# A hand-written TensorE order: both sums of a unit pair in even units, one place per unit for full-size work, D x u one unit later

## The chip, the cores and the metric

One core of a Trainium2 chip runs the kernel. The metric is the device time of one execution in microseconds (us). All arithmetic of the kernel is fp32.

## What is computed

The reference is a "macaron" block over x of shape (16, 512, 256): half a feed-forward layer, a selective state-space (Mamba-like) mixer, and half a feed-forward layer again. Cut to what matters here:

```python
x = x + 0.5 * ffn(layernorm(x))
# mixer: u = silu(conv(h @ Win[:, :512])), z = h @ Win[:, 512:], dt = softplus(u @ dt_w + dt_b)
#        Bt = u @ Bp, Ct = u @ Cp        (512 channels, 64 states per channel, 512 time steps)
def step(state, inp):
    x_t, dt_t, B_t, C_t = inp
    dA = jnp.exp(dt_t[:, :, None] * A[None])
    state = state * dA + (dt_t * x_t)[:, :, None] * B_t[:, None, :]
    y_t = jnp.einsum('bds,bs->bd', state, C_t)
    return (state, y_t)
y = (y + u * D) * silu(z)
x = x + (x_ + y @ Wout)
x = x + 0.5 * ffn(layernorm(x))
```

## The kernel before

**Units.** The mixer's state is walked in units. A unit is one tile of 128 channels with four of the 64 states, over all 512 time steps. A sequence of the batch has 64 units (`GN`), and 16 sequences follow one another. Units `n` and `n + 1` (`n` even) are a pair: the same four states for two neighbouring channel tiles. `HALF` is 32: the first 32 units serve channel tiles 0 and 1, the last 32 serve tiles 2 and 3. Each unit goes through four engines:

- ScalarE makes `dA` (L435), four exponentials of 128x512, into a ring of two.
- TensorE makes `pUB`, the product of dt x u and B, by 64x64 tiles (`force`, L687). It does so in two halves `i = 0, 1` of two states each; each half is 32 matmul records. There is one PSUM buffer per half, so half `i` of a unit may start only when VectorE has read half `i` of the unit before (`state_done`, L679).
- VectorE runs the recurrence (`tensor_tensor_scan`, L567): four scans per unit, two per half, each half waiting for `forced`. It writes `H`, a ring of four units.
- GpSimd multiplies `H` by C in place (L602), one operation of 128x1024 per half.
- TensorE adds the products into `Y` in PSUM by 64x64 tiles with an identity (`add_states`, L713). One call covers half of the states (two of four) of both units of a pair: 16 matmul records. Its second call frees the pair's places in `H` (`summed`, L716), which VectorE waits for four units later.

**D x u** (`skip_over`, L701) opens the accumulation of `Y`: two calls per 32 units, one per channel tile. They wait until VectorE has gated the earlier content of `Y` (`gate`, L547), which itself waits until all 32 units are summed.

**Everything else on TensorE** is full-size (128x128) work of the neighbouring sequences, since three are in flight: the scanned one `b`, the projections of `b + 1`, the first feed-forward of `b + 2`, and the closing of `b - 1`. Tables of unit numbers (`PES`, `LATER`, L38 to L42) put it in small pieces into the function `other` (L745): from unit 4 to unit 46 every unit has exactly one piece, after that only units 48, 50, 53, 56 and 58 and, next, 0 and 2. The pieces called on below are those of `project` (L635), `convolve` (L642), `project_u` (L648), `turn_b` (L660), `turn_u` (L668), `transpose` (L721), `feed_forward` (L730 to L732, L726) and `give_back` (L739, L726).

**The order of TensorE** is written out by hand in `step` (L818 to L840) and is a single in-order stream. In step `n` both halves of `force` are for unit `n + 1`, one unit ahead of VectorE. Before, an even step was: half 0 of `force`, second sum of the pair before, half 1 of `force`, `other`. An odd step was: half 0 of `force`, `other`, half 1 of `force`, first sum of the present pair (its first unit is done and the first half of its second).

**SyncE's queue** issues all DMAs, in an order by unit as well (L334 onward). At every even unit it loads the next pair's B diagonals (`Bd`, L289) and C rows (`Cb`, L292). The C load waits until GpSimd has finished all units before `n`. At unit 25 the B values of sequence `b + 1` are stored as pairs of numbers on diagonals (`store_diagonals`, L303, eight DMAs). The block that TensorE needs from unit 28 on is loaded right behind that, at unit 26.

Of the kernel before, what the change touches and what calls it, by code (L numbers as in the profile page):

```python
# [16 lines left out]
GN = NBLK * KI  # L17
HALF = GN // 2
# [27 lines left out]
def at(n):  # L46

    return START + n
# [168 lines left out]
def layers(nc, sb, pb, sem, counters, c, dram):  # L217
# [63 lines left out]
    with nc.Block() as block:  # L281
# [349 lines left out]
        def _(pe):  # L631
# [60 lines left out]
            def skip_over(b, n):  # L692

                k = 2 * (n // HALF) + n % 2
                pe.wait_ge(u_done, at(KI * b + k + 1))
                pe.wait_ge(u_kept, at(2 * b + max(k - 1, 0)))
                pe.wait_ge(gated, at(KI * b + k // 2 * 2))
                pe.sem_inc(pe_go, 1)
                for r in range(2):
                    rows, side = slice(r * HP, r * HP + HP), slice(k % 2 * HP, k % 2 * HP + HP)  # L700
                    last = nc.tensor.matmul(Y[r][side, :], c["diagD"][rows, k, rows], U[rows, k, :] if k < 2 else U2[rows, k - 2, :],  # L701
                                            start=True, stop=False)
                last.then_inc(skip, 1)

            def add_states(b, n, half):

                pe.wait_ge(times_c, at(2 * (GN * b + n + 1) + half + 1))
                pe.sem_inc(pe_go, 1)
                for j in (2 * half, 2 * half + 1):
                    for r in range(2):  # L710
                        rows = slice(r * HP, r * HP + HP)
                        for i in range(2):
                            last = nc.tensor.matmul(Y[r][i * HP:i * HP + HP, :], c["ident"][rows, rows], H[rows, (n + i) % HR, j, :],  # L713
                                                    start=False, stop=(n % HALF == HALF - 2 and j == GS - 1))
                if half:
                    last.then_inc(summed, 2)  # L716
# [101 lines left out]
            def step(b, scan, close, proj, ffn):  # L818
                for n in range(GN):
                    if scan and n + 1 < GN:  # L820
                        force(b, n + 1, 0)
                    if proj and n + 1 == GN:
                        force(b + 1, 0, 0)
                    if n % 2:
                        other(b, n, close, proj, ffn)
                    if scan and n % 2 == 0 and n:
                        add_states(b, n - 2, 1)
                    if close and n == 0:
                        add_states(b - 1, GN - 2, 1)
                    if scan and n + 1 < GN:  # L830
                        force(b, n + 1, 1)
                    if proj and n + 1 == GN:
                        force(b + 1, 0, 1)
                    if n % 2 == 0:
                        other(b, n, close, proj, ffn)
                    if scan and n % HALF == 1:
                        skip_over(b, n - 1)
                        skip_over(b, n)
                    if scan and n % 2:
                        add_states(b, n - 1, 0)  # L840

            steps(pe, step)


# [35 lines left out]
```

## Time and profile before

| | |
|---|---|
| median of 3 runs | 6116.61 us (6114.18 to 6119.97) |
| the profiled execution: its own time / its span | 6156.25 us / 6154.4 us |
| PE (matmul) busy | 5423.4 us, 88% |
| POOL (GpSimd) busy | 5101.6 us, 83% |
| DVE (VectorE) busy | 4829.4 us, 78% |
| ACT (ScalarE) busy | 4068.8 us, 66% |
| mean granted TensorE clock | 0.948 |

Busy time counts an engine as busy while a record of it lies open; the rest is waiting or issue time. No engine is at 100%, so the kernel is bound by different engines in different stretches, and the rows of the timeline tell which. Names in the rows: PE is a matmul, PEld a weight load, SPq the queue of DMA issues. `L687` is a line of the kernel. In the timeline the first number is the start in us from the span's beginning, the second the length of the (merged) entry.

### The profile page before, as it was taken

What the parts mean: (1) busy time and instruction counts of PE and PEld (TensorE: products, weight loads), DVE (VectorE), ACT (ScalarE), POOL (GpSimd) and SP (SyncE); (2) the same over time, 40 slices, a digit from 0 to 9 for tenths busy, and PEclk for the clock granted to TensorE, in tenths of its full rate; (3) what the DMA queues carried; (4) which work ended last, traced back from release to release, by engine and by line L of the source; (5) the groups of instructions that cost most, each with busy time, mean ns of one, the idle gap of its engine ahead of it and who ended that gap; (6) DMA issues with size and microseconds to landing.
All of it is one profiled execution on the core that took longest, in us unless ns stands there. A gap on an engine that the chain in (4) does not pass through costs nothing.

```text
span 6154.4 us, 207624 instructions
## 1 busy us (share of the span) xinstructions
PE 5423.4 (88%) x86664; PEld 3375.6 (55%) x86664; DVE 4829.4 (78%) x4323; ACT 4068.8 (66%) x6785; POOL 5101.6 (83%) x2326
## 2 busy tenths in 40 slices
PE   5888889888898988899888998888988889898887
PEld 2455555555565555555555565555655556555554
DVE  0679787787887878788787887878778788797996
ACT  3767576666766667576675766657666676766664
POOL 0779798887988879798797988979888798897996
PEclk9899999999999999999999999999999999999999
DMA  5566665666656666666665656656566666655553
GB/s 132 199 153 222 145 212 171 169 202 153 208 156 188 202 157 208 155 187 199 161 209 150 197 194 157 210 143 209 176 170 206 148 213 156 190 189 142 191 179 112
DMA packets 650457, 1095.40 MB, mean 178 GB/s; under 512 B 302817, under 2 KB 336386, under 8 KB 583938
## 3 DMA queue, kind: packets, MB, share of 16 engines
q1 hardware_dynamic: 649474, 1081.40, 60.9%
q8 instruction: 726, 11.89, 0.8%
q14 instruction: 257, 2.11, 0.1%
HBM read 875.74 MB, written 205.52 MB: 176 GB/s over the span
## 4 chain that ended last, share of the span: by engine, by line
POOL 52%; issue 23%; PE 10%; SPq 6%; DMA 5%; DVE 1%; ACT 1%; POOLq 1%; DVEq 0%; ACTq 0%
POOL H L602 49%; SPq L303 6%; DMA Cb<-scratch_c 4%; PE pUB L687 3%; PE Y L713 3%; DVE H L567 1%; POOL lnv L616 1%; POOL dto L620 1%; PE pP L642 1%; PE pP L648 1%; SPq L289 1%; PE pP L635 1%; POOLq L601 0%; DMA Bd<-scratch_diag 0%; POOL X L626 0%
## 5 line engine op out<-in xcount | busy, mean ns | idle before, releaser
L567 DVE TENSOR_TENSOR_SCAN H<-dA,pUB 128x512 f32<-128x512 f32 x4096 | 4698.3, 1203 | 1108.8 <-PE pUB L687 1061.6
L602 POOL TENSOR_TENSOR H<-H,Cb 128x1024 f32<-128x1024 f32 x2048 | 4814.8, 2387 | 824.1 <-DVE H L567 815.7
L435 ACT ACTIVATE dA<-DT,w_negA 128x512 f32<-128x512 f32 x4096 | 2615.3, 710 | 1134.5 <-DVE H L567 1121.6
L687 PEld LDWEIGHTS pUB<-Bd,UT 64*64 64x64 f32 x65536 | 1975.6, 136 | 1560.5 <-issue 1547.5
L687 PE MATMUL pUB<-Bd,UT 64*64 64x128 f32 x65536 | 2303.3, 277 | 556.5 <-DMA Bd<-scratch_diag 247.1
L713 PE MATMUL Y<-H,w_ident 64*64 64x512 f32 x16384 | 2026.9, 605 | 69.4 <-POOL H L602 63.1
L713 PEld LDWEIGHTS Y<-H,w_ident 64*64 64x64 f32 x16384 | 660.6, 137 | 658.2 <-issue 649.4
L435 ACT ACT_TABLE_LOAD x224 | 287.4, 1283 | 4.0
L408 ACT ACTIVATE absv<-pP,w_dt_b 128x512 f32<-128x512 f32 x64 | 44.0, 687 | 358.3 <-PE pP L648 358.3
L635 PE MATMUL pP<-hT,w_Win 128*128 128x512 f32 x512 | 264.4, 641 | 16.0 <-ACT uto L423 12.7
L648 PE MATMUL pP<-U,w_dt_w 128*128 128x512 f32 x512 | 270.9, 655 | 3.4 <-ACT zo L399 3.4
L642 PE MATMUL pP<-xs,w_taps 128*128 128x512 f32 x512 | 252.9, 617 | 4.2 <-ACT xs L386 2.9
L386 ACT ACTIVATE xs<-pP 128x512 f32<-128x512 f32 x64 | 38.3, 598 | 180.2 <-PE pP L635 180.2
L576 DVE SCALAR_TENSOR_TENSOR ev<-ev,absv 128x512 f32<-128x512 f32 x64 | 90.5, 1414 | 80.2 <-ACT ev L418 80.2
L732 PE MATMUL pA<-w_Wf,XNT 128*128 128x256 f32 x512 | 151.0, 419 | 0.0
L648 PEld LDWEIGHTS pP<-U,w_dt_w 128*128 128x128 f32 x512 | 93.5, 203 | 99.9 <-issue 99.9
L616 POOL TENSOR_TENSOR lnv<-lnv,ev 128x512 f32<-128x512 f32 x64 | 81.5, 1273 | 80.5 <-DVE ev L576 80.5
L635 PEld LDWEIGHTS pP<-hT,w_Win 128*128 128x128 f32 x512 | 89.6, 195 | 105.0 <-issue 100.0
L642 PEld LDWEIGHTS pP<-xs,w_taps 128*128 128x128 f32 x512 | 86.8, 188 | 90.9 <-issue 86.4
L739 PE MATMUL pA<-w_Wout,YG 128*128 128x256 f32 x512 | 127.4, 392 | 2.2 <-DVE YG L547 1.4
L660 PE MATMUL pP<-w_bc_w,U 128*128 128x64 f32 x512 | 127.4, 422 | 0.3 <-ACT U L394 0.3
L660 PEld LDWEIGHTS pP<-w_bc_w,U 128*128 128x128 f32 x512 | 121.8, 329 | 8.0 <-issue 7.4
(85 smaller groups left out, 2350.3 us busy)
## 6 DMA issues: line engine op xcount, KB each, us to landing
Cb<-scratch_c SPq DMA_DIRECT2D x512, 1024.0 KB, 5.5
Bd<-scratch_diag SPq DMA_DIRECT2D x512, 512.0 KB, 4.5
scratch_diag<-blank SPq DMA_DIRECT2D x512, 256.0 KB, 5.9
scratch_z<-zo SPq DMA_DIRECT2D x64, 256.0 KB, 6.3
scratch_dt<-dto SPq DMA_DIRECT2D x64, 256.0 KB, 6.4
scratch_ut<-uto SPq DMA_DIRECT2D x64, 256.0 KB, 7.4
DT<-scratch_dt SPq DMA_DIRECT2D x64, 256.0 KB, 5.3
UT<-scratch_ut SPq DMA_DIRECT2D x64, 256.0 KB, 6.6
```

The source lines that it names most:

```text
L303: sp.dma_start(spot, BT[r * HP:r * HP + HP, j, :].rearrange("p (i s) -> p i s", s=2)).then_inc(d_st, 16)
L435: last = nc.scalar.activation(dA[:, n % DAR, j, :], DT[:, k, :], ACT.Exp, scale=c["negA"][:, k, GS * blk + j:GS * blk + j + 1])
L567: last = nc.vector.tensor_tensor_scan(H[:, n % HR, 2 * i + j, :], dA[:, n % DAR, 2 * i + j, :], pUB[:, i, :].rearrange("p (t s) -> p s t", ...
L602: nc.gpsimd.tensor_tensor(h[:, j:j + 2, :], h[:, j:j + 2, :], Cb[:, blk % 2, j:j + 2, :], ALU.mult).then_inc(times_c, 1)
L616: nc.gpsimd.tensor_tensor(lnv[:, :], lnv[:, :], ev1[:, :], ALU.subtract).then_inc(soft2, 1)
L635: last = nc.tensor.matmul(pP[:, :], c["Win"][:, k, col + m * P:col + (m + 1) * P], hT[:, k, :], start=(k == 0), stop=(k == KM - 1))
L642: last = nc.tensor.matmul(pP[:, :], c["taps"][:, m, j, :], xs[:, m % 2, j:j + T], start=(j == 0), stop=(j == DC - 1))
L648: last = nc.tensor.matmul(out, weight[:, k, lo:lo + width], U[:, k, :], start=(k == 0), stop=(k == KI - 1))
L660: last = nc.tensor.matmul(pP[:, j * DS:(j + 1) * DS], columns(U[:, k, :], j), c["bc_w"][:, k, 0:DS], start=(k == 0), stop=(k == KI - 1))
L687: last = nc.tensor.matmul(out, UT[rows, k, j * P + h * HP:j * P + h * HP + HP], Bd[rows, blk % 2, i, j * P:(j + 1) * P].rearrange("p (t s) ...
L713: last = nc.tensor.matmul(Y[r][i * HP:i * HP + HP, :], c["ident"][rows, rows], H[rows, (n + i) % HR, j, :], start=False, stop=(n % HALF == ...
L732: nc.tensor.matmul(pA[:, j, :], XNT[:, k, lo:lo + P], c["Wf"][:, k, :], start=False, stop=False)
```

## The change

Only TensorE's order changes. In every unit `other` now stands between half 0 and half 1 of `force`. Both sums of a pair stand together at the end of the even step behind half 1 of `force`; the odd step ends with half 1. D x u moves from the end of odd steps 1 and 33 to even steps 2 and 34, between `other` and half 1 of `force`.

```diff
@@ -821,23 +821,19 @@
                         force(b, n + 1, 0)
                     if proj and n + 1 == GN:
                         force(b + 1, 0, 0)
-                    if n % 2:
-                        other(b, n, close, proj, ffn)
-                    if scan and n % 2 == 0 and n:
-                        add_states(b, n - 2, 1)
-                    if close and n == 0:
-                        add_states(b - 1, GN - 2, 1)
+                    other(b, n, close, proj, ffn)
+                    if scan and n % HALF == 2:
+                        skip_over(b, n - 2)
+                        skip_over(b, n - 1)
                     if scan and n + 1 < GN:
                         force(b, n + 1, 1)
                     if proj and n + 1 == GN:
                         force(b + 1, 0, 1)
-                    if n % 2 == 0:
-                        other(b, n, close, proj, ffn)
-                    if scan and n % HALF == 1:
-                        skip_over(b, n - 1)
-                        skip_over(b, n)
-                    if scan and n % 2:
-                        add_states(b, n - 1, 0)
+                    for half in range(2):
+                        if scan and n % 2 == 0 and n:
+                            add_states(b, n - 2, half)
+                        if close and n == 0:
+                            add_states(b - 1, GN - 2, half)
 
             steps(pe, step)
 
```

The instructions of ScalarE, VectorE and SyncE's queue are the same, in the same order; GpSimd's work is too. The first place shown is TensorE, loop body, units 6 to 8 (`L687` is a half of `force`, `L713` a sum, `L739` with `L726` a piece of `give_back`, `L642` a convolution; 64x512 x8 is one call of `add_states`). Before:

```order
L687 MATMUL pUB<-Bd,UT 64x64x2 x16
L713 MATMUL Y<-H,w_ident 64x512 x8
L687 MATMUL pUB<-Bd,UT 64x64x2 x16
L739 MATMUL pA<-w_Wout,YG 128x256 x4
L726 MATMUL pA<-X,w_ident 128x256
L687 MATMUL pUB<-Bd,UT 64x64x2 x16
L642 MATMUL pP<-xs,w_taps 128x512 x2
L687 MATMUL pUB<-Bd,UT 64x64x2 x16
L713 MATMUL Y<-H,w_ident 64x512 x8
```

and after the change:

```order
L687 MATMUL pUB<-Bd,UT 64x64x2 x16
L739 MATMUL pA<-w_Wout,YG 128x256 x4
L726 MATMUL pA<-X,w_ident 128x256
L687 MATMUL pUB<-Bd,UT 64x64x2 x16
L713 MATMUL Y<-H,w_ident 64x512 x16
L687 MATMUL pUB<-Bd,UT 64x64x2 x16
L642 MATMUL pP<-xs,w_taps 128x512 x2
L687 MATMUL pUB<-Bd,UT 64x64x2 x16
```

The two sums, before at two places with a half of `force` between them, are one block of twice the length, and the even unit's full-size piece has moved ahead of half 1 of `force`.

The second place is TensorE at the loop's start, units 0 to 2 (`L701` is D x u, `L635` a projection). Before:

```order
L687 MATMUL pUB<-Bd,UT 64x64x2 x16
L713 MATMUL Y<-H,w_ident 64x512 x8
L687 MATMUL pUB<-Bd,UT 64x64x2 x16
L635 MATMUL pP<-hT,w_Win 128x512 x2
L687 MATMUL pUB<-Bd,UT 64x64x2 x32
L701 MATMUL Y<-U,w_diagD 64x512 x4
L713 MATMUL Y<-H,w_ident 64x512 x8
```

and after the change:

```order
L687 MATMUL pUB<-Bd,UT 64x64x2 x16
L635 MATMUL pP<-hT,w_Win 128x512 x2
L687 MATMUL pUB<-Bd,UT 64x64x2 x16
L713 MATMUL Y<-H,w_ident 64x512 x16
L687 MATMUL pUB<-Bd,UT 64x64x2 x48
L635 MATMUL pP<-hT,w_Win 128x512 x2
L701 MATMUL Y<-U,w_diagD 64x512 x4
```

Where a unit has no full-size piece, three halves of `force` now follow one another (x48), and D x u stands behind unit 2's projection.

## Rows read from the trace of the kernel before

**Rows 1.** Waits of the whole span: engine, line, waited for, us, times, longest.
```profile
DVE H L567 <- PE pUB L687: 1061.6, 1097, 19.3
...
PE pUB L687 <- DMA Bd<-scratch_diag: 247.1, 18, 17.6
...
PE Y L713 <- POOL H L602: 63.1, 73, 3.8
```

**Rows 2.** Timeline of TensorE, one loaded pair (steps 6 and 7).
```profile
2471.34 1.05 PE L687 MATMUL pUB<-Bd,UT 64*64 64x128 f32 x32
2472.22 1.90 PE L713 MATMUL Y<-H,w_ident 64*64 64x512 f32 x16
2473.93 1.05 PE L687 MATMUL pUB<-Bd,UT 64*64 64x128 f32 x32
2474.92 1.99 PE L739 MATMUL pA<-w_Wout,YG 128*128 128x256 f32 x8
...
2477.27 1.10 PE L687 MATMUL pUB<-Bd,UT 64*64 64x128 f32 x32
2478.31 1.99 PE L642 MATMUL pP<-xs,w_taps 128*128 128x512 f32 x4
2480.22 1.10 PE L687 MATMUL pUB<-Bd,UT 64*64 64x128 f32 x32
2481.15 1.90 PE L713 MATMUL Y<-H,w_ident 64*64 64x512 f32 x16
```

**Rows 3.** Timeline, a light pair (steps 56 and 57): TensorE, then VectorE.
```profile
2395.84 1.08 PE L687 MATMUL pUB<-Bd,UT 64*64 64x128 f32 x32
...
2402.12 1.10 PE L687 MATMUL pUB<-Bd,UT 64*64 64x128 f32 x32 [0.98 <-DVE H L567]
2403.01 1.93 PE L713 MATMUL Y<-H,w_ident 64*64 64x512 f32 x16
2404.73 1.08 PE L687 MATMUL pUB<-Bd,UT 64*64 64x128 f32 x32
...
2399.67 15.64 DVE L567 TENSOR_TENSOR_SCAN H<-dA,pUB 128x512 f32<-128x512 f32 x14
```

**Rows 4.** Timeline of TensorE, first of steps 28, 46, 62, 14, 20; half 1 in step 22.
```profile
2241.35 1.05 PE L687 MATMUL pUB<-Bd,UT 64*64 64x128 f32 x32
...
2342.35 1.08 PE L687 MATMUL pUB<-Bd,UT 64*64 64x128 f32 x32
...
2423.65 1.08 PE L687 MATMUL pUB<-Bd,UT 64*64 64x128 f32 x32
...
2517.42 1.05 PE L687 MATMUL pUB<-Bd,UT 64*64 64x128 f32 x32
...
2547.99 1.05 PE L687 MATMUL pUB<-Bd,UT 64*64 64x128 f32 x32
...
2568.46 1.04 PE L687 MATMUL pUB<-Bd,UT 64*64 64x128 f32 x32
```

**Rows 5.** Timeline of GpSimd, the DMA queue and TensorE around the B diagonals.
```profile
2571.99 2.36 POOL L602 TENSOR_TENSOR H<-H,Cb 128x1024 f32<-128x1024 f32 x1 [0.24 <-DVE H L567]
...
2575.67 23.84 SPq L303 DMA_DIRECT2D scratch_diag<-BT  x8
...
2610.45 1.98 PE L687 MATMUL pUB<-Bd,UT 64*64 64x128 f32 x32 [16.58 <-DMA Bd<-scratch_diag]
```

**Rows 6.** Timeline, two long gaps of TensorE: step 50, and the loop's jump back.
```profile
2364.32 1.99 PE L687 MATMUL pUB<-Bd,UT 64*64 64x128 f32 x32 [3.16 <-DVE H L567]
...
2436.70 1.98 PE L687 MATMUL pUB<-Bd,UT 64*64 64x128 f32 x32 [3.96 <-issue]
```

**Rows 7.** Timeline of GpSimd and VectorE after unit 49, one softplus operation.
```profile
2345.06 16.32 POOL L602 TENSOR_TENSOR H<-H,Cb 128x1024 f32<-128x1024 f32 x7
...
2357.95 3.98 DVE L576 SCALAR_TENSOR_TENSOR ev<-ev,absv 128x512 f32<-128x512 f32 x1
```

**Rows 8.** Timeline of VectorE, last sequence, a light pair.
```profile
5951.20 9.12 DVE L567 TENSOR_TENSOR_SCAN H<-dA,pUB 128x512 f32<-128x512 f32 x8 [0.16 <-PE pUB L687]
```

## The prediction

> **What bounds the kernel now.** I read the list of waits first, then the timeline of TensorE and VectorE through one loop iteration, and last the queue of DMA issues. The waits [rows 1] say who is late: VectorE stands idle 1061.6 us for TensorE's `pUB`. TensorE itself waits little for others: 247.1 us for B diagonals in 18 long pieces, 63.1 us for GpSimd. So what counts is the time at which TensorE delivers each half of `force`.
>
> The timeline shows three regimes. In a *loaded* pair (both units with a full-size piece of about 2 us) TensorE never stops [rows 2]. From start to start a half costs 0.87 us before a sum, 0.98 to 1.04 before full-size work and 0.93 behind it; a call of sums costs 1.72; the two pieces here 2.35 and 1.91. The sum is 0.88 + 1.71 + 0.99 + 2.35 + 1.04 + 1.91 + 0.93 + 1.71 = 11.52 us for a pair. TensorE is the bound.
>
> In a *light* pair [rows 3] TensorE waits 0.98 us for VectorE and the pair takes 2404.73 - 2395.84 = 8.89 us. VectorE is the bound: 14 chained scans in 15.64 us are 2.23 us for a half, four halves are 8.9.
>
> Third, **the B diagonals** once per sequence [rows 5]. GpSimd ends unit 23 at 2574.35, the queue then gives out the eight diagonal stores in 23.84 us, and the block for unit 28 waits behind them: TensorE stands until 2610.45. From the end of unit 23 to the first half of unit 28 there are 36.1 us of DMA time, whatever TensorE does meanwhile. Steps 24 to 27 are therefore free of charge, and a sequence costs (unit 28 to unit 23 of the next) + 36.1.
>
> **The change part by part.** Nothing is added or removed: the same matmuls stand in another order, and each engine's DMAs are untouched. In a loaded pair there are as many passages between tile sizes as before, so TensorE's own sum stays at 11.5 us and costs nothing. What changes is when a half of `force` can be delivered.
>
> *Both sums together.* Half 1 of `force` for the pair's first unit may start only when VectorE ends half 1 of the unit before. Then two calls of sums follow, and only then half 0 for the next unit. Follow that ring with the measured pieces [rows 3]: 0.1 from VectorE's end to TensorE's start (2399.67 + 2.3 against 2402.12), 0.9 for the half, 2 x 1.72 = 3.4 for the sums, 1.15 for half 0 and its signal, then two halves on VectorE, 4.5. That is 10.1 to 10.2 us per pair. VectorE has work for 4.5 us of the first 5.6 and idles 1.1. Before, with one call of sums between any two halves, no ring was longer than VectorE's own 8.9. So each pure light pair loses 1.3 us.
>
> *The even full-size piece ahead of half 1.* It puts the piece E into a ring of its own: half 0, E, half 1, two sums, half 0, VectorE's half: 0.1 + 1.0 + E + 0.9 + 3.4 + 1.15 + 2.3 = 8.9 + E. An odd piece O gives the same, 8.9 + O. With 1.9 us in only one of the two units that is 10.8 us, where TensorE's sum (7.1 + E + O) or VectorE gave 9.1 to 9.8. With both pieces loaded the ring is 10.8 to 11.3, under TensorE's 11.0 to 11.5, so these pairs stay.
>
> Through one loop iteration, walked pair by pair with these three bounds [rows 4]:
>
> - steps 28 to 46, before 101.0 us. Seven pairs are loaded; three (two short transposes, or one beside a full piece) lose about 1 us each. Against that, the first sum no longer asks GpSimd for the unit just scanned, which gives back the 2.9 us of such waits in these steps, and the order after the stall brings 1.7 us of sums behind the start point, with about 0.7 more from smaller waits: -2.3.
> - steps 46 to 62, before 81.3 us, eight pairs. Four pure light pairs +1.3, less 0.8 for one that already holds a gap; step 46 with one projection +1.6; steps 48 to 53 are stretched already and gain about 0.6: +6.6.
> - steps 62 to 14, before 93.8 us. Light steps 62, 0 and 2, of which 2 has its projection *and* D x u (0.87 us) in the ring, cost some 4.1 us, less 0.5 at the jump, because the 3.96 us gap [rows 6] now begins without a sum ahead of it. Steps 4 to 12 are loaded; TensorE starts them without the waits that it had there, -2.3: +1.3.
> - steps 14 to 20, before 30.6 us, three pairs. Steps 16 and 18 hold one transpose (0.6) and one convolution: 9.8 to 10.85: +2.2.
> - steps 20 to 22, before 20.5 us. The two `turn_b` pieces of 3.9 us slow the clock behind each; half 1 of step 22 now has a feed-forward piece instead of a sum ahead of it: +1.3.
> - the rest is hidden by the 36.1 us [rows 5]: 0. What hides it is the 16.58 us of waiting there; a loss beyond that would show.
>
> Sum: **+9.1 us per sequence**, 14 times (sequence 0 to sequence 14): 127 us. Sequence 0 up to unit 23 lacks the closing pieces, so 10 pairs are light or half loaded: +12. Sequence 14 behind unit 28 lacks the feed-forward pieces: +9. Sequence 15 is almost all light, at 9.12 + 0.16 = 9.28 us per pair [rows 8]; 32 pairs x 0.9: +29. Together +177 us.
>
> D x u itself costs nothing more: VectorE's gates are over when TensorE reaches step 34, where before it could wait for them.
>
> The profiled execution took 6156 us by itself and would take 6333; the median of the runs shown, 6117, is 40 us (0.6%) below it. I add the difference to the median: **6294 us**, 2.9% slower.
>
> Bounds: the ring is longer than VectorE's 8.9 by 1.3 in light pairs for certain if the rows hold. The loaded pairs are the unknown: their rings have 0.1 to 0.6 us to spare. If none of the losses outside pure light pairs came (4 pairs and the seam per sequence, plus sequence 15) the sum would be 14 x 5 + 29 = 100, so 6217. If half of the 23 loaded and half-loaded pairs lost 0.5 us more, 14 x 5.5 = 77 more: 6371.
>
> **A port.** After unit 49 the softplus operation on VectorE took 3.98 us, while GpSimd ran without a gap until 2361.38, and it ended 0.55 us behind that run [rows 7]. In the new order GpSimd has gaps of about 0.2 us per half in such pairs, but the two products of unit 49 still stand back to back, so I keep about 4 us. If the gaps let it in at once, up to 3.3 us in each of 13 sequences, 43 us, come back. The Trainium skill (GPSIMD Engine Reference, 1. Specifications) says that GpSimd's SBUF interfaces are shared with VectorE, with contention for VectorE operations with two SBUF inputs; by that rule the time falls with GpSimd's density, and the trace agrees with the contention.
>
> **The rivals.**
>
> 1. *Forecast*: the ring through the two sums binds. For it: arithmetic from rows, and VectorE already depends on TensorE's delivery [rows 1]. 0.76.
> 2. *The ring binds but the port opens* (above), and the gap of step 50 shrinks with it: 14 x 6 + 50 = 134, near 6250. 0.10.
> 3. *Faster.* The sums come a unit later and ask GpSimd for nothing fresh, so the 63.1 us of waits [rows 1] go, and TensorE, waiting less, runs far enough ahead to hide the long block. It would give 6117 - 63 = 6054. Against it: half 1 cannot start before VectorE frees its buffer, so TensorE can't run ahead. It decides if the block of sums is under 2.3 us, not 3.4. 0.05.
> 4. *No change.* TensorE's sum binds nearly everywhere and losses in light pairs are made up by its backlog: 6117. Against it: the 8.89 us pair with a waiting TensorE [rows 3]. 0.05.
> 5. *The clock falls.* Behind waits of 3.16 and 3.96 us a half takes 1.99 and 1.98 us instead of 1.10 [rows 6], half of the full clock; behind 0.98 us it doesn't [rows 3]. The new order has waits of up to 1.8 us in light pairs. Should the clock go to 1.2 GHz there, the ring's 5.4 us of TensorE double: 5 us x 5 pairs x 14 = 350 more, about 6640. The Trainium skill (TensorE: Matmul & The Clock Gate, What's actually happening) holds that the default is the throttled state and that activity releases it; the rows at either length of wait agree. 0.04.
>
> **How the numbers follow.** 6294 is the first case. The range 6200 to 6380 takes in cases 1 and 2 with the bounds 6217 and 6371; left out are cases 3, 4, 5 and a little of case 1. A measurement of this kernel tells about 0.2% from no change. Faster by more 0.05 (case 3), same 0.05 (case 4), slower 0.90.
>
> **What would show it.** Light pairs at 10.1 to 10.2 us between starts of even steps, with VectorE waiting about 1.1 us once per pair for the half behind the sums; loaded pairs at 11.5; single-piece pairs near 10.8; TensorE's waits for GpSimd's `H` gone; VectorE's wait for `pUB` up from 1061.6 by about 180; the wait for `Bd` still 14 to 17 us. Light pairs at 8.9 would make the ring wrong; loaded pairs above 11.8 would mean rings that I did not see; a granted clock below 0.93 would mean case 5.

## The result, and the profile after

The changed kernel takes **6413.95 us** (median of 4 runs, 6402.3 to 6432.65), beside 6118.29 us for the kernel before on the same chip (6114.18 to 6120.64). The ratio is 1.0487, 95% interval [1.0459, 1.0515]: slower, as forecast, but by 296 us where 177 were forecast, and outside the range of 6200 to 6380.

The page of the profiled execution, busy times and costliest groups:

```profile
span 6430.8 us, 207624 instructions
...
PE 5490.6 (85%) x86664; PEld 3406.3 (53%) x86664; DVE 4808.4 (75%) x4323; ACT 4075.1 (63%) x6785; POOL 5090.4 (79%) x2326
...
L576 DVE SCALAR_TENSOR_TENSOR ev<-ev,absv 128x512 f32<-128x512 f32 x64 | 112.8, 1762 | 80.3 <-ACT ev L418 80.3
```

The work is the same and every engine is busy for a smaller share of a longer span, so most of the loss is waiting. (TensorE's own busy time is 67 us above its 5423.4 us of before, with the same matmuls: some of them ran slower.) Which waiting, the list of waits says (engine, line, waited for, us, times, longest):

```profile
DVE H L567 <- PE pUB L687: 1366.9, 806, 16.0
...
PE pUB L687 <- DVE H L567: 527.4, 376, 4.8
PE pUB L687 <- DMA Bd<-scratch_diag: 199.1, 16, 13.5
...
DVE YG L547 <- PE Y L713: 34.5, 32, 4.9
...
PE Y L713 <- POOL H L602: 0.7, 2, 0.4
```

VectorE's wait for `pUB` rose by 305 us from the 1061.6 of [rows 1], in fewer and longer pieces, and TensorE's wait for VectorE from 212.5 to 527.4 us. When each of two engines waits more for the other, a ring between them (a closed chain in which each waits for the other's last result) has probably become longer. TensorE's wait for GpSimd [rows 1] is gone, as the forecast said; it was worth little.

A loaded pair like that of [rows 2], here units 12 and 13 (VectorE, then TensorE):

```profile
2603.06 2.33 DVE L567 TENSOR_TENSOR_SCAN H<-dA,pUB 128x512 f32<-128x512 f32 x2 [1.35 <-PE pUB L687]
...
2614.58 2.33 DVE L567 TENSOR_TENSOR_SCAN H<-dA,pUB 128x512 f32<-128x512 f32 x2 [1.35 <-PE pUB L687]
...
2605.28 1.98 PE L687 MATMUL pUB<-Bd,UT 64*64 64x128 f32 x64
2607.18 1.98 PE L635 MATMUL pP<-hT,w_Win 128*128 128x512 f32 x4
2609.10 1.10 PE L687 MATMUL pUB<-Bd,UT 64*64 64x128 f32 x32
2610.02 3.61 PE L713 MATMUL Y<-H,w_ident 64*64 64x512 f32 x32
```

TensorE has no gap and the pair takes 2614.58 - 2603.06 = 11.52 us, exactly as before. Light pairs like that of [rows 3], in the last sequence, where many follow one another:

```profile
6187.62 9.00 DVE L567 TENSOR_TENSOR_SCAN H<-dA,pUB 128x512 f32<-128x512 f32 x8 [1.27 <-PE pUB L687]
6197.89 9.00 DVE L567 TENSOR_TENSOR_SCAN H<-dA,pUB 128x512 f32<-128x512 f32 x8 [1.27 <-PE pUB L687]
...
6200.37 1.10 PE L687 MATMUL pUB<-Bd,UT 64*64 64x128 f32 x32 [1.76 <-DVE H L567]
6202.59 1.10 PE L687 MATMUL pUB<-Bd,UT 64*64 64x128 f32 x32 [1.12 <-DVE H L567]
6203.49 3.64 PE L713 MATMUL Y<-H,w_ident 64*64 64x512 f32 x32
```

9.00 us of scans and one wait of 1.27 us behind the block of sums (3.64 us) make 10.27 us, where 8.89 to 9.28 stood before [rows 3, 8]. Forecast: 10.1 to 10.2 with one wait of 1.1.

What the forecast did not have is in the same view of the seventh sequence (unit 56) and of a later one (units 35 to 37):

```profile
2876.36 1.98 PE L687 MATMUL pUB<-Bd,UT 64*64 64x128 f32 x32 [1.66 <-DVE H L567]
2878.27 1.11 PE L721 MATMUL pA<-w_ident,XN 128*128 128x128 f32 x4
...
3929.07 4.19 DVE L576 SCALAR_TENSOR_TENSOR ev<-ev,absv 128x512 f32<-128x512 f32 x1
...
3935.65 1.99 PE L687 MATMUL pUB<-Bd,UT 64*64 64x128 f32 x32 [3.41 <-DVE H L567]
3937.57 3.75 PE L635 MATMUL pP<-hT,w_Win 128*128 128x512 f32 x4
```

In the first, a half takes 1.98 us instead of 1.10 and a transpose 1.11 instead of 0.66: the granted clock of this half is 0.50, so TensorE is at 1.2 GHz, the lower of its two levels, behind a wait of 1.66 us. In the second, `ev`, one elementwise operation of the softplus, stands 4.19 us behind unit 35; before, it took 0.67 us there and about 4 only behind unit 49 [rows 7]. TensorE then waits 3.41 us for VectorE and comes back at half speed, for the half and for most of the projection.

To place the loss I took the start of the first scan of every even unit from both traces. Averages over sequences 1 to 13, in us from one even unit to the next (these and all "periods" below are differences of such starts):

| even unit | before | after | | even unit | before | after |
|---|---|---|---|---|---|---|
| 2 | 9.86 | 12.77 | | 48 | 12.83 | 13.68 |
| 8, 10, 12, 14 | 11.41 | 11.41 | | 50 | 12.82 | 12.18 |
| 16 | 10.38 | 10.89 | | 54 | 9.33 | 11.12 |
| 34 | 10.04 | 11.94 | | 56 | 9.08 | 12.34 |
| 36 | 9.18 | 11.95 | | 58 | 8.95 | 10.32 |
| 38 | 12.69 | 11.28 | | 60 | 9.50 | 11.38 |

### The profile page after: what moved, and what is told of

Read it like the earlier page. It is cut to its first block, busy times and chain, and to the rows that moved or that the text cites. A ratio compares the mean times of both kernels' runs of the same rounds, so it can differ in the third digit from the quotient of the medians.

```text
span 6430.8 us, 207624 instructions
## 1 busy us (share of the span) xinstructions
PE 5490.6 (85%) x86664; PEld 3406.3 (53%) x86664; DVE 4808.4 (75%) x4323; ACT 4075.1 (63%) x6785; POOL 5090.4 (79%) x2326
## 4 chain that ended last, share of the span: by engine, by line
POOL 39%; PE 26%; issue 18%; DVE 7%; SPq 5%; DMA 2%; ACT 1%; POOLq 0%; DVEq 0%; ACTq 0%
POOL H L602 38%; PE Y L713 9%; PE pUB L687 9%; DVE H L567 7%; SPq L303 5%; PE pP L648 3%; DMA Bd<-scratch_diag 2%; PE pP L635 2%; PE pA L732 1%; PE pP L642 1%; PE pA L730 1%; PE pA L726 1%; POOL lnv L616 0%; PE pP L660 0%; POOLq L601 0%
## 5 line engine op out<-in xcount | busy, mean ns | idle before, releaser
L687 PE MATMUL pUB<-Bd,UT 64*64 64x128 f32 x65536 | 2270.1, 281 | 818.1 <-DVE H L567 527.4
L687 PEld LDWEIGHTS pUB<-Bd,UT 64*64 64x64 f32 x65536 | 1954.8, 138 | 1579.1 <-issue 1563.9
L713 PE MATMUL Y<-H,w_ident 64*64 64x512 f32 x16384 | 1894.3, 596 | 17.6 <-issue 16.8
L713 PEld LDWEIGHTS Y<-H,w_ident 64*64 64x64 f32 x16384 | 671.4, 135 | 847.5 <-issue 828.1
L635 PE MATMUL pP<-hT,w_Win 128*128 128x512 f32 x512 | 306.2, 729 | 16.0 <-ACT uto L423 12.7
L642 PE MATMUL pP<-xs,w_taps 128*128 128x512 f32 x512 | 252.9, 617 | 4.2 <-ACT xs L386 2.9
L576 DVE SCALAR_TENSOR_TENSOR ev<-ev,absv 128x512 f32<-128x512 f32 x64 | 112.8, 1762 | 80.3 <-ACT ev L418 80.3
L635 PEld LDWEIGHTS pP<-hT,w_Win 128*128 128x128 f32 x512 | 104.4, 226 | 127.0 <-issue 121.9
L642 PEld LDWEIGHTS pP<-xs,w_taps 128*128 128x128 f32 x512 | 86.8, 188 | 90.9 <-issue 86.4
L739 PE MATMUL pA<-w_Wout,YG 128*128 128x256 f32 x512 | 127.4, 392 | 2.2 <-DVE YG L547 1.4
L732 PEld LDWEIGHTS pA<-w_Wf,XNT 128*128 128x128 f32 x512 | 91.2, 198 | 52.9 <-issue 45.1
```

The costliest lines, as they stand in the source:

```text
L635: last = nc.tensor.matmul(pP[:, :], c["Win"][:, k, col + m * P:col + (m + 1) * P], hT[:, k, :], start=(k == 0), stop=(k == KM - 1))
L642: last = nc.tensor.matmul(pP[:, :], c["taps"][:, m, j, :], xs[:, m % 2, j:j + T], start=(j == 0), stop=(j == DC - 1))
L687: last = nc.tensor.matmul(out, UT[rows, k, j * P + h * HP:j * P + h * HP + HP], Bd[rows, blk % 2, i, j * P:(j + 1) * P].rearrange("p (t s) ...
L732: nc.tensor.matmul(pA[:, j, :], XNT[:, k, lo:lo + P], c["Wf"][:, k, :], start=False, stop=False)
L739: nc.tensor.matmul(pA[:, j, :], YG[:, k, (i * PAIR + j) * P:(i * PAIR + j + 1) * P], c["Wout"][:, k, :], start=(k == 0), stop=False)
```

## The experiments

The theory was the forecast's ring, together with the question what makes it cost more than its sum. All kernels are variants of the two by a few lines. Each ratio is to the kernel before on the same chip; on the four chips its median was 6112.73 to 6123.79 us, so a difference of two times from different chips is uncertain by some 10 us. The code cuts are shortened; `...` stands for lines left out.

**e1: the sums together, nothing else moved.** Kernel before, both sums behind half 1, even piece behind them:

```diff
-                    if scan and n % 2:
-                        add_states(b, n - 1, 0)
+                    for half in range(2):
+                        if scan and n % 2 == 0 and n:
+                            add_states(b, n - 2, half)
...
+                    if n % 2 == 0:
+                        other(b, n, close, proj, ffn)
```

> The kernel before, with one part of the change alone: both sums of a pair stand together behind half 1 of force in even units; the even full-size piece stays behind them, D x u stays at the end of units 1 and 33. Ring theory (a block of TensorE work between half 1 of one unit and half 0 of the next makes VectorE wait): the block is now two sums AND the even piece, so the ring of a pair is 0.1 + 0.9 + 3.4 + E + 1.15 + 4.5 = 10.1 + E: light pairs 10.2 us, pairs with a 1.9 us even piece 12.0, also the loaded ones that were at 11.5 or less. About 28 us more per sequence, some 6500 to 6560 us. Rival (the new order makes TensorE's own work slower, by passages between tile sizes or by issue gaps, and the place of the even piece matters little): at most the change's own 6414, and loaded pairs stay at 11.5.

Measured: 6888.2 us, ratio 1.1253 [1.1232, 1.1274]. The direction was right, the size far off, and TensorE's timeline of this kernel shows why:

```profile
2743.45 1.10 PE L687 MATMUL pUB<-Bd,UT 64*64 64x128 f32 x32 [1.67 <-DVE H L567]
2745.67 1.10 PE L687 MATMUL pUB<-Bd,UT 64*64 64x128 f32 x32 [1.12 <-DVE H L567]
2746.57 3.64 PE L713 MATMUL Y<-H,w_ident 64*64 64x512 f32 x32
2750.14 1.98 PE L642 MATMUL pP<-xs,w_taps 128*128 128x512 f32 x4
2752.05 1.10 PE L687 MATMUL pUB<-Bd,UT 64*64 64x128 f32 x32
2753.09 1.98 PE L642 MATMUL pP<-xs,w_taps 128*128 128x512 f32 x4
```

With the even piece behind the sums, sums, even piece, half 0, odd piece and half 1 follow one another without a half of VectorE between them, so *both* pieces E and O stand in one ring: 8.9 + E + O = 8.9 + 2 x 2.0 = 12.9; measured periods of loaded pairs 12.98 and 13.42, where my expectation had only one piece in it. Light pairs again 10.17. The expectation missed by over 300 us, and the ring with both pieces was written down after the result; the rows bear it out. Loaded pairs did not stay at 11.5, which speaks against the rival. Moving the even piece ahead of half 1 was then the part of the change that *limited* the damage of the double sum: 6414 with it, 6888 without.

**e2: the even piece ahead of half 1, sums at their old places.**

```diff
-                    if n % 2:
-                        other(b, n, close, proj, ffn)
+                    other(b, n, close, proj, ffn)
```

(the call of `other` behind half 1 is gone, so the second sum now stands behind the piece).

> The kernel before, with another part alone: the even full-size piece moves ahead (half 0, piece, second sum, half 1); the sums stay apart. Ring theory: light pairs keep 8.9 us; a pair with an even piece of 1.9 us has the ring 0.1 + 1.0 + 1.9 + 1.7 + 1.15 + 4.55 = 10.4 us, which is above VectorE's 9.3 only in the four or five pairs of a sequence whose odd unit has little, so 5 us per sequence: 6150 to 6200 us. Rival (the piece ahead of half 1 is what costs): most of the change's 296 us, above 6300.

Measured: 6299.11 us, ratio 1.0289 [1.0269, 1.0310]: a miss, at the 6300 from which the rival was to count. Piece and sum now stand in one ring in the even unit too: unit 36 has 10.56 (before 9.18), where 10.4 was expected; the lightest pairs keep 8.89. But fuller pairs lost as well (unit 32 13.90, before 12.29; unit 2 11.71, before 9.86), which the expectation had not. TensorE's wait for GpSimd is 92.2 us (63.1 before), since the first sum still asks for the unit just scanned; how the rest comes about is not shown. So either half of the change alone costs, and in different pairs.

**e3: the changed kernel with the first sum back at the end of the odd unit.**

```diff
-                    for half in range(2):
-                        if scan and n % 2 == 0 and n:
-                            add_states(b, n - 2, half)
+                    if scan and n % 2 == 0 and n:
+                        add_states(b, n - 2, 1)
...
+                    if scan and n % 2:
+                        add_states(b, n - 1, 0)
```

(the closing sums and D x u are likewise where they were before).

> The changed kernel with the first sum put back at the end of odd units (and D x u before it): half 0, piece, half 1, one sum, in every unit. The sums are apart again, all else is the change. Ring theory: no block between two halves is longer than one sum or one piece, the whole loss goes: light pairs 8.9, loaded 11.5, 6080 to 6140 us, about the kernel before. Rival (the place of the even piece, or clock and issue gaps that come with the new order): stays above 6250.

Measured: 6129.92 us, ratio 1.0012 [1.0001, 1.0023], as expected. The even piece still stands in its new place. One row of VectorE's timeline:

```profile
2713.96 9.00 DVE L567 TENSOR_TENSOR_SCAN H<-dA,pUB 128x512 f32<-128x512 f32 x8 [0.26 <-PE pUB L687]
```

The gap ahead of the 9.00 us of scans is 0.26 us. The distance to the kernel before on the same chip is 6 us, where the change had 296: with the first sum back in its place, and D x u with it, nearly all of the loss is gone. It takes the two sums in one block to make it. The difference from e2 is the order of piece, half 1 and second sum: here piece, half 1, sum; there piece, sum, half 1.

**e4: the gates out of the ring.** Changed kernel, `gate` (L547) of units 2 and 34 behind the first half of that unit's scans:

```diff
-                    if scan and n == HALF + 2:
-                        gate(b, 0)
-                        gate(b, 1)
...
                             last.then_inc(state_done, 1)
+                            if n == HALF + 2 and i == 0:
+                                gate(b, 0)
+                                gate(b, 1)
```

> The changed kernel; VectorE's two pairs of gates (units 2 and 34) now stand behind the first half of that unit's scans instead of ahead of it. If the gates' wait (0.7 to 1.3 us) and their 1.3 us stand in the ring of the pairs at units 2, 34 and 36, as the trace of the change suggests and the prediction denied, 3 to 4 us per sequence come back: about 6350 to 6370 us, and those pairs fall to about 10.6 to 11. If they are covered, the time stays at 6414.

Measured: 6430.82 us, ratio 1.0488 [1.0452, 1.0523], the same as the changed kernel. Unit 2 improved (12.77 to 11.76), unit 34 got worse (11.94 to 12.71). In the changed kernel unit 2 takes 11.75 us in five of the 13 sequences and 13.4 in the eight in which TensorE falls to the lower clock; here it takes 11.76 in all 13 and the clock stays at 1.00. So the gates do matter in unit 2, but moving them gives nothing back in the sum.

**e5: both sums in the even unit, but not together**; the even unit's piece goes into the odd unit.

```diff
-                    if n % 2:
-                        other(b, n, close, proj, ffn)
                     if scan and n % 2 == 0 and n:
-                        add_states(b, n - 2, 1)
+                        add_states(b, n - 2, 0)
...
+                    if n % 2:
+                        other(b, n - 1, close, proj, ffn)
```

(the second sum stands behind half 1, the odd piece behind half 1 of the odd unit).

> Sums a unit later as in the change, but apart: even unit half 0, first sum, half 1, second sum; odd unit half 0, the even unit's full-size piece, half 1, the odd unit's piece. Ring theory: no block between two halves is longer than one sum or one piece, so light pairs keep 8.9 us and loaded ones 11.5; TensorE no longer asks GpSimd for a fresh product, so its 63 us of such waits go: 6050 to 6110 us, faster than the kernel before. Against it: both pieces come half a unit later and ScalarE or the scans could wait for them, then 6120 or more. If 'sums a unit later' were itself the cost, near 6414.

Measured: 6276.72 us, ratio 1.0272 [1.0257, 1.0286]: a miss. Its rings are short (light pairs 8.9 again), but every piece comes later, the even ones by half a unit or more, and ScalarE, which reads these pieces in a fixed order with `dA`, comes late with it. One of its waits, and then the timeline of ScalarE, VectorE and TensorE around unit 42:

```profile
DVE H L567 <- ACT dA L435: 232.4, 169, 2.7
```

```profile
2729.49 0.60 ACT L472 ACTIVATE X<-pA 128x512 f32<-128x512 f32 x1 [4.62 <-PE pA L726]
...
2733.11 2.77 DVE L576 SCALAR_TENSOR_TENSOR ev<-ev,absv 128x512 f32<-128x512 f32 x1 [0.21 <-ACT ev L418]
2737.09 6.78 DVE L567 TENSOR_TENSOR_SCAN H<-dA,pUB 128x512 f32<-128x512 f32 x6 [1.21 <-ACT dA L435]
...
2739.57 1.10 PE L687 MATMUL pUB<-Bd,UT 64*64 64x128 f32 x32 [3.06 <-DVE H L567]
```

VectorE waited 28.5 us for `dA` before, 232.4 here. ScalarE stands 4.62 us for a full-size piece, its exponentials slip, `ev` waits and then VectorE waits for `dA`; TensorE is idle 3.06 us in a stretch that was full. In this kernel full-size work can't be moved later for TensorE's sake alone.

**e6 and e7: half of the sums left out.** e6 is the kernel before without its first sum (`add_states(b, n - 1, 0)`), e7 the changed kernel with `for half in (1,)`. In both, two of the four states of each unit are not added into `Y`.

> The kernel before without the first sum of each pair (two of the four states of every block are left out of Y; nothing else is left out). TensorE's sum of a loaded pair falls from 11.5 to 9.8 us, light pairs stay at 8.9 to 9.3. About 28 us less per sequence: 5680 to 5780 us. It is the control for the next run.

> The changed kernel without the first sum of each pair (the same two of four states left out). The block between half 1 and the next half 0 is now one sum, 1.7 us, so every ring is 1.7 us shorter: light pairs 8.4, under VectorE's 8.9, pieces 7.2 + 1.9 = 9.1, under TensorE's 9.8. Ring theory: the distance of 296 us to the kernel before falls to under 60 us when both are cut. Rival (the new order costs in itself, by tile passages, the moved piece or D x u): the distance stays above 200 us.

Measured: 5915.0 us (0.9676) and 5906.91 us (0.9666). The distance of the two orders fell from 296 us to -8 us. The places of the piece and of D x u in e7 are those of the change, so they cost nothing when the block is one sum. Both kernels have less work on TensorE than a full one and could hide more, so e3, which leaves nothing out, is the stronger test; the two agree. The absolute times missed: 203 us saved in e6, not 340 to 440. The waits of e6 say that much of the work taken from TensorE came back as waiting for VectorE (212.5 us before), and its clock was 0.913 (before 0.948):

```profile
PE pUB L687 <- DVE H L567: 546.2, 483, 5.3
```

**e8: the changed kernel with work added.** In units 49 to 63 one unread full-size product of 256 columns wherever TensorE had a wait:

```diff
+                if 49 <= n < 56:
+                    pe.wait_ge(o_done, at(2 * b))
+                    nc.tensor.matmul(pA[:, 0, :], c["ident"][:, :], c["Win"][:, 0, 0:DM], start=True, stop=True)
```

(from 57 on the same into `pP`; called in odd units and in 52, 54, 60 and 62, of sequences that have both neighbours).

> The changed kernel with one extra full-size product of 256 columns (about 0.45 us, nobody reads it) in the idle stretches of TensorE in the light units: at the end of odd units 49 to 63 and between the halves of even units 52, 54, 60 and 62, in the 13 loop iterations. It adds work on an engine. If the clock's falls behind waits are what makes light pairs 11 to 12 us instead of the 10.2 of the ring, the clock stays at 1.00 there, pairs 54 to 62 go to 10.2 to 10.4 and the time to 6350 to 6390 us. If clock falls don't matter, or the rest is issue gaps, it stays at 6414 or rises by up to 60 us.

Measured: 6345.39 us, ratio 1.0378 [1.0362, 1.0394], mean clock 0.956: **69 us faster than the changed kernel by doing more** (65 by the distances on the two chips), and 5 us below the expected range. A view by stretches (us, busy PE, PEld, DVE, ACT, POOL, then PEclk, DMA share, GB/s), the pair of unit 56 in the changed kernel, then in this one, and two rows of this one's timeline (L823 is the added product):

```profile
2874.00:2886.50 12.50, 9.80 (x173) 6.79 (x168) 8.95 (x8) 7.27 (x13) 9.68 (x5) 0.86 0.59 171
```

```profile
2836.00:2846.00 10.00, 8.45 (x167) 5.55 (x163) 9.00 (x8) 6.14 (x11) 8.93 (x5) 1.00 0.68 210
```

```profile
2836.78 0.70 PE L823 MATMUL pA<-w_Win,w_ident 128*128 128x256 f32 x2
2838.49 1.10 PE L687 MATMUL pUB<-Bd,UT 64*64 64x128 f32 x32 [1.01 <-DVE H L567]
```

With 0.70 us of product ahead of it the wait is 1.01 us, the half takes 1.10 us and the granted clock is 1.00, where it was 0.86. In the trace's clock records TensorE was at the lower level for 10.8 us of units 46 to 61 in an average sequence of the changed kernel, and for 1.8 us here. The periods of units 56, 58, 60, 62 are 10.17, 10.17, 10.21, 10.18 on average (changed kernel 12.34, 10.32, 11.38, 10.59): the ring's own length and no more. Unit 54 was expected there too and stayed at 11.25. The Trainium skill (TensorE: Matmul & The Clock Gate, What's actually happening) says that activity is what releases the throttled state; this run agrees, with 10.8 against 1.8 us.

**e9, e10, e12: without the operation `ev`.** The third suspect was GpSimd and VectorE in each other's way. e9 is the kernel before, e10 the changed one, e12 is e8, each without this operation; left out is the rounding correction of the softplus.

```diff
-                nc.scalar.activation(ev1[:, :], absv[:, :], ACT.Copy, bias=1.0).then_inc(one_done, 1)
+                nc.scalar.activation(ev1[:, :], absv[:, :], ACT.Copy, scale=0.0).then_inc(one_done, 1)
...
-                        nc.vector.scalar_tensor_tensor(out=ev1[:, :], in0=ev1[:, :], scalar=-1.0, in1=absv[:, :],
...
-                        pool.wait_ge(soft1, at(s + 1))
+                        pool.wait_ge(one_done, at(s + 1))
```

> The kernel before, without VectorE's operation ev (L576) and with ScalarE writing zeros into ev; what is left out is the rounding correction of the softplus. VectorE loses 64 operations of 90.5 us in total; 12 of them, behind unit 49, took 3.97 to 4.00 us each, and TensorE waited 3.16 us behind one. Contention theory (ev behind unit 49 stands in the way of the ring, its own length and the slow clock after the gap are paid): 12 x 4 to 7 us fewer, with little for the others, which lie in pairs bound by TensorE: 6030 to 6070 us. Rival (these operations lie beside waits anyway, the price is nothing): 6105 to 6120 us.

> The changed kernel without the same operation ev, ScalarE writing zeros into ev; the rounding correction of the softplus is left out. After the change ev behind unit 35 took 1.85 or 4.2 us (before: 0.67) and behind unit 49 0.96 to 4.5 us. Contention theory (the new order puts ev behind unit 35 beside a GpSimd without gaps, and pair 36 pays for it, 11.95 us on average and 10.89 at best): this kernel gains what the one before gains and 1 to 2.5 us more in each of 13 sequences, pair 36 falls to 10.9, 6300 to 6350 us. Rival (the excess of pairs 34 and 36 comes from the ring and the gates alone): it gains no more than the kernel before does, and pair 36 stays near 12 us.

> The changed kernel without ev (the same rounding correction is left out) and with the unread products of e8_filled in the idle stretches of units 49 to 63. If the clock behind idle stretches and the ev operation are two separate parts of the excess over the forecast, both gains add: 69 us from the products and the gain of e10_after_no_ev, 6240 to 6290 us, and the distance to the kernel before without ev is 200 to 240 us, which the ring alone has to explain (177 in the forecast). If they are one and the same part (the clock fell because ev made the gaps), this kernel is within 15 us of the better of e8_filled and e10_after_no_ev.

Measured: e9 6054.55 us (0.9893 [0.9876, 0.9911]), e10 6363.0 us (1.0396 [1.0378, 1.0415]), e12 6304.94 us (1.0312 [1.0293, 1.0331]), all beside 6112.73 us for the kernel before on their chip. e9 confirms the price: 58 us for an operation whose 64 instances would take 43 us at 0.67 each, most of them beside waits. e10 is split. The pairs did what the contention theory said (units 34 and 36 fell to 10.52 and 10.90 and no longer vary). VectorE in this kernel, where L684 is the line that was L687:

```profile
2725.67 8.99 DVE L567 TENSOR_TENSOR_SCAN H<-dA,pUB 128x512 f32<-128x512 f32 x8
2736.19 9.00 DVE L567 TENSOR_TENSOR_SCAN H<-dA,pUB 128x512 f32<-128x512 f32 x8 [1.53 <-PE pUB L684]
```

But the total gain of 51 us misses the expected range of 6300 to 6350 us and is no larger than the 58 of the kernel before: leaving `ev` out shortens units 28 to 45 of an average sequence by 3.3 us in the changed order and by 0.6 in the old one, units 46 to 61 by 0.6 and by 1.7. So the new order moved a cost and did not add one. e12 missed its range by 15 us (and the distance to e9, 250 us, the expected 200 to 240); it is 58 us under e10, so the clock's part and `ev`'s part are nearly separate.

**e11: a try for a faster kernel.** Before `ev` of unit 49 [rows 7] GpSimd ran without a gap for some 33 us, with `X + XA` of unit 44 in the middle. Kernel before with

```diff
-POOLS = {"dt": (30, 35, 42, 49), "r": (44,)}
+POOLS = {"dt": (30, 35, 42, 49), "r": (49,)}
```

> The kernel before with GpSimd's operation of 2.4 us X + XA (L626) moved from behind unit 44 to behind unit 49, after the softplus. GpSimd ran without a gap from that operation on (23.29 us of products) until it met ev. If this operation is what takes GpSimd's gaps away, ev behind unit 49 falls from 4 us to 2 or less, the wait of 3.16 us behind it shrinks with it, and the kernel takes 6065 to 6100 us, faster than both. If GpSimd is full there in any case, or the 2.4 us come back as a wait of TensorE for H in unit 50, it stays at 6110 to 6130 us.

Measured: 6100.3 us (12 runs, 6094.35 to 6116.7) beside 6112.73, ratio 0.9980 [0.9969, 0.9991]. VectorE and GpSimd:

```profile
2709.62 1.04 DVE L576 SCALAR_TENSOR_TENSOR ev<-ev,absv 128x512 f32<-128x512 f32 x1
...
2703.12 9.77 POOL L602 TENSOR_TENSOR H<-H,Cb 128x1024 f32<-128x1024 f32 x4 [0.57 <-DVE H L567]
...
2716.86 2.37 POOL L626 TENSOR_TENSOR X<-X,XA 128x1024 f32<-128x1024 f32 x1
...
2726.31 1.95 PE L713 MATMUL Y<-H,w_ident 64*64 64x512 f32 x16 [1.40 <-POOL H L602]
```

`ev` fell from 4 us to 1.05 in sequences 1 to 13, as the first theory wanted, but TensorE's wait for GpSimd rose from 63.1 to 97.9 us, as the second did. The time lies on the upper bound of the first range. The balance is a gain of 0.2%, 12 us, at the edge of what can be told; it is the only version without anything left out that was below the kernel before.

The first theory's reason does not hold, though. The row of GpSimd shows one run without a gap from 2703.12 to 2712.89, and `ev` took 1.04 us in the middle of it. What the traces show is when `ev` ends. Here are GpSimd's products around the `ev` behind unit 35 of the changed kernel, in the seventh sequence and then in that of the 4.19 us shown above:

```profile
2755.99 2.38 POOL L602 TENSOR_TENSOR H<-H,Cb 128x1024 f32<-128x1024 f32 x1
2757.06 1.85 DVE L576 SCALAR_TENSOR_TENSOR ev<-ev,absv 128x512 f32<-128x512 f32 x1
...
3927.99 2.41 POOL L602 TENSOR_TENSOR H<-H,Cb 128x1024 f32<-128x1024 f32 x1
3930.31 2.40 POOL L602 TENSOR_TENSOR H<-H,Cb 128x1024 f32<-128x1024 f32 x1
```

The first `ev` ends at 2758.91, 0.54 us behind the end of the product in which it began (2758.37). The second ends at 3933.26, 0.55 us behind the end of the *next* product (3932.71). So it is in all eleven profiles that have the operation: of 480 `ev` that began while a GpSimd operation ran, 347 ended about 0.55 us behind the end of that one, 125 behind the second end and 8 behind the third; 224 began beside an idle GpSimd and took 0.7 us. In e11 it was the first end instead of the second. Both kinds occur in runs without a gap, and what decides between them is not shown.

## Why the prediction was wrong in size, point by point

- **The ring of the light pair: right.** 10.17 to 10.27 us measured, 10.1 to 10.2 forecast. e3 (sum back, +0.1%) and e7 (block halved, -8 us against e6) show that the double sum is the cause.
- **Loaded pairs unchanged: right.** 11.52 and 11.08 us in both, units 8 to 14.
- **Sums of the forecast.** They add up as stated. Two slips don't enter the total: steps 28 to 46 are nine pairs, not seven and three, and the +6.6 of steps 46 to 62 comes out only if the 0.6 us that steps 48 to 53 "gain" is a loss.
- **Steps 24 to 27 free: right.** Unit 24 to unit 28 took 36.2 us after. The profiled execution of before shows 39.2 there, but e9 and e11, whose order on TensorE is the same, 36.6 and 36.3. So (39.2 - 36.4) x 14 = 39 us of that execution's 40 us over the median probably lie in this stretch of DMA time; the same kernel was not profiled twice. Adding the difference to the median and not to the profile was then sound.
- **"The clock falls", rival 5: one step that failed.** I made it one case for all light pairs, with a chance of 0.04 and a cost of 350 us, and put the clock behind the new waits at nothing in the sum. In the traces it is partial: behind the regular gaps of 1.76 and 1.12 us in the last sequence the halves keep 1.10 us, while at 2876.36 one wait of 1.66 us is followed by half speed, and the mean clock of the run hardly shows it (0.946 against 0.948). The length of one wait does not decide it. Counted ahead of unbroken halves, the trace of before had 91 waits of TensorE for VectorE of 1.1 to 1.6 us, of which 2 were followed by a slow half (over 1.5 us), and none of 1.6 to 1.9 us. After the change there are 130 of 1.6 to 1.9 us, 12 of them followed by a slow half, and even of the 53 of 0.5 to 0.9 us 9 are; my line "behind 0.98 us it doesn't" is no rule. Its price is the 65 to 69 us of e8 (58 without `ev`), for units 49 to 63 alone; it belonged in the sum as a term with a range, not in a rival.
- **The port: half right.** I had `ev` fixed behind unit 49 at about 4 us. It went from there to 0.96 to 4.5 us, varying by sequence, and appeared behind unit 35 at 1.85 or 4.2. In the sum this came out even (51 us against 58), but only by luck. Nor is it GpSimd's density that sets the length, as I had it, but the end of a GpSimd operation (e11).
- **The gains set against the rings: the other step that failed.** e9 and e12 have no `ev`, and e12 has hardly any slow clock in units 46 to 61 (1.6 us per sequence). They come nearest to the rings alone. Us per loop sequence (1 to 13), from the starts described above:

| stretch | forecast | after - before | e12 - e9 |
|---|---|---|---|
| units 28 to 46 | -2.3 | +2.8 | +0.1 |
| 46 to 62 | +6.6 | +9.4 | +5.6 |
| 62 to 14 | +1.3 | +4.4 | +4.6 |
| 14 to 20 | +2.2 | +1.2 | +1.2 |
| 20 to 24 | +1.3 | +0.5 | +1.7 |
| 24 to 28 | 0 | -3.0 | -1.2 |
| sum | +9.1 | +15.3 | +12.0 |

  Where light pairs make up the stretch (46 to 62) the ring terms held. What did not come in full were the gains that I set against them. In units 28 to 46 I had losses of 3 us against gains of 5.3 us (the "2.9 us of such waits" for GpSimd and 2.4 more); in e12 less e9 the pairs of units 34 and 36 lose 2.4 us and units 28, 32 and 38 give back 2.5. In units 4 to 12 I had a gain of 2.3 us and there is a loss of 0.8, nearly all of it in unit 4 (10.15 to 10.91 after the change); the pairs from unit 6 on were at 11.1 to 11.5 already. My reading is that TensorE was at its sum there, so that a wait removed from the middle of a full pair moves the next one; no run tests it by itself. In unit 2 the forecast's own ring, 8.9 + 1.9 + 0.87 = 11.7, is the shortest period seen (11.75); in 8 of 13 sequences it is 13.4, with the clock at 0.55 in the projection (3.45 us, not 1.9):

```profile
2547.11 1.10 PE L687 MATMUL pUB<-Bd,UT 64*64 64x128 f32 x32 [2.21 <-DVE H L567]
2548.14 3.45 PE L635 MATMUL pP<-hT,w_Win 128*128 128x512 f32 x4
```

- **"D x u itself costs nothing more: VectorE's gates are over when TensorE reaches step 34": wrong in its reason.** The last sum before a gate is now the end of the double block, and the gate waits for it. VectorE's waits at `gate` went from one of 6.8 us to 32 with 34.5 us in all. In unit 34 this wait and the gates themselves stand ahead of the scans:

```profile
2746.95 1.29 DVE L547 TENSOR_TENSOR YG<-Y,ZL 128x512 f32<-128x512 f32 x2 [0.69 <-PE Y L713]
```

  By e4 moving them pays nothing in all, so what they cost by themselves stays open.
- **Sequences 0, 14 and 15.** By the forecast's own division: sequence 0 up to unit 23, forecast +12, measured +10; sequence 14 behind unit 28, +9 and +9; sequence 15, +29 and +40. The 14 loops, forecast +127, measured +219 between the two profiled executions, although that of before was slower in steps 24 to 27. In sequence 15 a light pair of before took 8.89 to 9.3, not always 9.28, and 10.27 after; pairs with one full piece went from 8.9 to 10.1 up to 11.1 to 11.9 in most cases, not 10.8.

In medians: e12 less e9 is 250 us, where the forecast's rings and gains came to 177. e10 less e12, the fills in the changed kernel, is 58. The rest is `ev`, 51 - 58 = -7. The three add up to 301, the distance of 6413.95 to 6112.73, by the way they are formed; that is no test of them. And the 250 is not the rings alone. The slow clock outside units 49 to 63 is still in both kernels, and e9 was not filled: in unit 52 of its seventh sequence TensorE waits 3.5 us for GpSimd and comes back at half clock, and unit 52 takes 13.2 to 15.0 us in sequences 1 to 13. If filling it gained time there as well, the rings' share would be larger and the clock's smaller; that was not run.

What stays open is why the lower clock takes one wait of 1.66 us and spares another of 1.76: the order of work ahead of them differs, but no run separated it. Filling units 0 to 3 and 34 to 37 wasn't tried.

## What to carry to other kernels

Where two engines hand halves of a buffer to each other, write out the ring (delivery, everything queued behind it, the other engine's half) before merging two blocks on one of them: here the merge cost nothing on TensorE's own sum (11.52 us in a loaded pair) and 1.3 us in the ring of every light pair. Be slow to subtract waits that vanish from a stretch in which that engine is already full: of the 7.6 us per sequence subtracted here some 2.5 came. And price the slower clock as a term wherever a change makes TensorE's waits longer in lightly loaded stretches; a few unread products there are a cheap test of it.

## What the runs showed of the hardware

- Adding 0.70 us products to TensorE's idle places made the kernel 65 to 69 us faster (e8), with a granted clock of 1.00 in place of 0.86 in a pair.
- The length of one wait did not tell whether the lower clock followed: after the change it did behind 12 of 130 waits of 1.6 to 1.9 us and behind 9 of 53 of 0.5 to 0.9 us.
- The same VectorE operation on two 128x512 fp32 tiles in SBUF took 0.67 us by itself and 0.67 to 7.1 us beside a GpSimd operation that read SBUF. It ended about 0.55 us behind the end of the GpSimd operation in which it began (347 of 480), or of the next (125) or the third (8). The Trainium skill (GPSIMD Engine Reference, 1. Specifications) names the contention for VectorE instructions with two SBUF inputs, which this one has; the rows give its size.
- Half of TensorE's sums left out (e6) saved only 203 us, with the clock at 0.913: much of the freed time became waiting (546.2 us for VectorE, before 212.5), and part of the rest ran at the lower clock.
